# A graph-attention edge stream on one core: all source rows of a chunk gathered by GpSimd, none picked by TensorE

## The reference, cut to what matters

```python
h = (x_flat @ W_gat).reshape(M, HEADS, NUM_EXPERTS)        # M = 16384 nodes, 4 x 4
src = concatenate([edge_index[0], loops])                  # 262144 edges and 16384 loops
dst = concatenate([edge_index[1], loops])
a_src = (h * att_src).sum(-1);  a_dst = (h * att_dst).sum(-1)
e = leaky_relu(a_src[src] + a_dst[dst], negative_slope=0.2)
e_max = segment_max(e, dst);  ee = exp(e - e_max[dst])
denom = segment_sum(ee, dst)
alpha = ee / (denom[dst] + 1e-16)
agg = segment_sum(h[src] * alpha[:, :, None], dst) + b_gat
...
hh = gelu(x @ W1[ei] + b1[ei]);  out += g * (hh @ W2[ei] + b2[ei])   # four experts
```

## Time and profile before

| | us |
|---|---|
| median of 3 runs | 5086.44 (5078.35 to 5090.78) |
| profiled execution, span from first to last instruction | 5093.1 |
| PE busy | 3045.9 (60%) |
| DVE busy | 2806.7 (55%) |
| ACT busy | 2362.3 (46%) |
| POOL busy | 2224.4 (44%) |
| L937, the picking matmuls, x13056 | 1835.9 |
| L857, the gathers of the stream, x1632 | 1548.1 |

### The profile page before, as it was taken

How to read it: one execution, slowest core, us unless ns; L and a number is a source line. 1 busy time by engine, 2 the same in 40 slices (tenths; PEclk the granted TensorE clock), 3 DMA queues, 4 the chain that set the end, 5 groups by cost and what they waited for, 6 DMA issues and landing times. The chain is left out here.

```text
span 5093.1 us, 63233 instructions
## 1 busy us (share of the span) xinstructions
PE 3045.9 (60%) x21149; PEld 2318.6 (46%) x21149; DVE 2806.7 (55%) x5784; ACT 2362.3 (46%) x4288; POOL 2224.4 (44%) x2218
## 2 busy tenths in 40 slices
PE   3656663666566566566566566566566566544775
PEld 2445542554454454455455455455455455432443
DVE  8857883445445445445445445445445445467986
ACT  3636655444444444444444444444434434404886
POOL 7865613334434434434434434434434434426530
PEclk7657775777777777777777777777777777766887
DMA  1111101111111111111111111111111111112101
GB/s 58 24 22 20 22 7 44 24 23 27 31 23 27 31 23 27 31 23 27 31 23 27 31 23 27 31 23 27 31 23 27 31 23 27 25 27 75 38 19 33
DMA packets 157528, 145.13 MB, mean 28 GB/s; under 512 B 71240, under 2 KB 133080, under 8 KB 156776
## 3 DMA queue, kind: packets, MB, share of 16 engines
q1 hardware_dynamic: 88656, 109.49, 6.4%
q0 software_dynamic: 68768, 34.45, 6.2%
HBM read 92.97 MB, written 50.82 MB: 28 GB/s over the span
## 5 line engine op out<-in xcount | busy, mean ns | idle before, releaser
L937 PE MATMUL es_pgot<-hash_space,es_pick 128*128 128x256 bf16 x13056 | 1835.9, 288 | 1423.7 <-issue 1418.8
L857 POOL DMA_INDIRECT es_got<-node_table,late x1632 | 1548.1, 949 | 2127.0 <-DVEq L1077 1649.7
L937 PEld LDWEIGHTS es_pgot<-hash_space,es_pick 128*128 128x128 bf16 x13056 | 1302.8, 101 | 1899.6 <-issue 1742.7
L1019 DVE TENSOR_TENSOR es_prod<-es_pgot,es_own 128x512 f32<-128x512 f32 x272 | 187.7, 690 | 1801.6 <-PE es_pgot L937 1627.7
L871 ACT ACTIVATE es_pick<-es_away,consts 128x512 bf16<-128x512 f32 x1088 | 680.0, 711 | 7.0 <-DMA es_away<-sorted_keys 6.6
L293 POOL DMA_INDIRECT fr_ring<-in_emb,fr_rows x384 | 456.0, 1188 | 209.8 <-issue 112.8
L875 ACT ACTIVATE es_pick<-es_pick,consts 128x4096 bf16<-128x4096 bf16 x136 | 503.6, 3703 | 0.9
L894 ACT ACTIVATE ex_hid<-ex_phid,weights 128x256 f32<-128x256 f32 x128 | 53.6, 470 | 692.7 <-PE ex_phid L944 692.3
L1039 DVE TENSOR_TENSOR es_hot<-es_iota,late 128x1024 bf16<-128x1024 f32 x272 | 331.7, 1219 | 33.4 <-DVE es_st L1079 25.7
L1040 DVE TENSOR_TENSOR es_hot<-es_iota,late 128x1024 bf16<-128x1024 f32 x272 | 330.2, 1214 | 0.0
L894 ACT ACT_TABLE_LOAD x32 | 41.1, 1283 | 559.2 <-PE ex_phid L944 559.2
(11 more groups left out here) (351 smaller groups left out, 4294.6 us busy)
## 6 DMA issues: line engine op xcount, KB each, us to landing
es_away<-sorted_keys SPq DMA_DIRECT2D x68, 512.0 KB
es_got<-node_table,late POOLq DMA_INDIRECT x1632
edge_states<-es_st SPq DMA_DIRECT2D x68, 384.0 KB
expert_outputs<-ex_y SPq DMA_DIRECT2D x64, 256.0 KB
bk_y<-expert_outputs SPq DMA_DIRECT2D x8, 2048.0 KB
fr_ring<-in_emb,fr_rows POOLq DMA_INDIRECT x384
out_dram<-h SPq DMA_DIRECT2D x4, 1024.0 KB, 5.1
late<-in_edges SPq DMA_DIRECT2D x1, 2048.0 KB, 9.3
```

The costliest lines, as they stand in the source:

```text
L857: pool.indirect_dma_start(out=got[:, r, k, :], out_offset=None, in_=table_dram, in_offset=bass.IndirectOffsetOnAxis(ap=src[:, n, k:k + 1]. ...
L937: mm = pe.matmul(p_got[:, q, c * 256:c * 256 + 256], pick[:, r, q // 2, k, at * P:at * P + P], parts[:, part, k], start=(k == 0 and part = ...
```

## The change

GpSimd gathers all 32 columns of each chunk. The picking goes away with all that served it: the table's parts and the four `split` calls in `front`, the index rows and their transfers through DRAM, ScalarE's one-hots, TensorE's `pair`, VectorE's `sides`, `take` and `scores`. The hash arrays of `front`, which lay in the space of the parts, now lie in the ring of embedding rows. VectorE waits for 32 landings of a buffer in place of 24. Everything else, in the remaining order, stays.

```diff
-pool_cols = lambda t: t.rearrange("p (n c) -> p n c", c=CH)[:, :, 0:GC]
-pe_cols = lambda t: t.rearrange("p (n c) -> p n c", c=CH)[:, :, GC:]
+by_chunk_cols = lambda t: t.rearrange("p (n c) -> p n c", c=CH)
...
-        low = hash_space[0:B]
+        rows = sb("rows", [P, TILES, 3], I32)
+        ring = sb("ring", [P, RINGS, 3, ST, D])
+        low = ring[0:B].rearrange("b r n t d -> b (r n t d)")
...
-            def split(j):
-
-                tiles = slice(j * 32, j * 32 + 32)
-                block_rows = tab[:, tiles, 0:16].rearrange("p (h k) f -> p k h f", k=BLOCKS)
...
-                    ch.step(v.tensor_scalar(src, pool_cols(key), M - 1, None, ALU.bitwise_and))
...
-                    ch.step(v.tensor_scalar(few, pe_cols(key), BLOCKS * P - 1, None, ALU.bitwise_and)); ch.settle()
-                    ch.step(v.tensor_copy(mem["within"], tmp[:, 0:ROWS_T])); ch.settle()
-                    ch.step(v.tensor_scalar(few, pe_cols(key), 10, SIDES - 1, ALU.logical_shift_right, ALU.bitwise_and)); ch.settle()
-                    ch.step(v.tensor_copy(side, few)); ch.settle()
+                    ch.step(v.tensor_scalar(src, by_chunk_cols(key), M - 1, None, ALU.bitwise_and))
...
-                    if r < loads:
-                        pause(sp, s_pick, i * 4 + r * 2 + 4, s_spent)
-                        load(i * 2 + r + 3, 1 - r)
...
-                for k in range(GC):
+                for k in range(CH):
                     pool.indirect_dma_start(out=got[:, r, k, :], out_offset=None, in_=table_dram,
...
-                    if r < picks:
-                        pause(act, s_away[r], i * 16 + 32, s_spent)
-                        pause(act, s_got_p, c * PAIRS + 2, s_spent)
-                        squares(r, 0)
...
-                    if r < pairs:
-                        pair(c + 1, 1 - r, 0)
                     if with_experts:
                         expert(c, 0)
                         expert(c, 1)
-                    if r < pairs:
-                        pair(c + 1, 1 - r, 1)
                     count(c, 0)
                     count(c, 1)
...
-                    pause(dve, s_landed[r], (i + 1) * (16 * GC), s_spent)
+                    pause(dve, s_landed[r], (i + 1) * (16 * CH), s_spent)
...
                     count(c, 0)
                     count(c, 1)
-                    if r < takes:
-                        sides(c + 1)
-                        take(c + 1, 1 - r, 0)
-                        take(c + 1, 1 - r, 1)
...
                     count(c, 2)
                     count(c, 3)
-                    if r < takes:
-                        take(c + 1, 1 - r, 2)
-                        take(c + 1, 1 - r, 3)
-                        scores(1 - r)
```

More of the change, by code:

```diff
@@ L590, in _ @@
             dve.sem_inc(s_sorted, 1)
-            src, side, keep, starts, drop, hi, lo = (mem[n] for n in ("src", "side", "keep", "starts", "drop", "hi", "lo"))
-            few = tmp[:, 0:ROWS_T].rearrange("p (n c) -> p n c", c=PC)
+            src, keep, starts, drop, hi, lo = (mem[n] for n in ("src", "keep", "starts", "drop", "hi", "lo"))
             def prepare(part):
@@ L777, in edge_stream @@
         ps = lambda name, shape: ctx.enter_context(nc.psum_tensor(name, shape, F32))
-        C, W, xts, parts = mem["C"], mem["W"], mem["xts"], mem["parts"]
-        src, side, keep, starts, drop, hi, lo, within = (mem[n] for n in ("src", "side", "keep", "starts", "drop", "hi", "lo", "within"))
-        away = sb("es_away", [P, 2, PC * P], F32)
+        C, W, xts = mem["C"], mem["W"], mem["xts"]
+        src, keep, starts, drop, hi, lo = (mem[n] for n in ("src", "keep", "starts", "drop", "hi", "lo"))
         hot = sb("es_hot", [P, 2, 2, OH, P], BF16)
[L782 to L786, removed]
         row0 = sb("es_row0", [P, ROW], F32)
@@ L862, in _, with turn @@
             a = nc.scalar
[L863 to L884 removed]
+            def turn(i, with_experts):
                 for r in range(2):
                     c = i * 2 + r
[L887 to L890 removed]
                     if with_experts:
@@ L922, in _ @@
             pe.matmul(counts, hot[:, 0, 0, 0, :], hot[:, 0, 1, 0, :], start=True, stop=False, skip_group_check=True).then_inc(s_used, 2)
-            for b in range(5):
-                n = min(P, ROWS_T - b * P)
-                mm = pe.transpose(p_got[:].rearrange("p q n -> p (q n)")[0:n, b * P:b * P + P], within[:, b * P:b * P + n], C("ident"))
-            mm.then_inc(s_turned_p, 1)
-            def pair(n, r, q, first=False):
-                if q % 2 == 0:
-                    pause(pe, s_pick, n * 2 + q // 2 + 1, s_spent)
-                if not first:
-                    pause(pe, s_taken, (n - 1) * PAIRS + q + 1, s_spent)
-                for c in range(2):
-                    at = (q % 2) * 2 + c
-                    for k in range(BLOCKS):
-                        for part in range(3):
-                            mm = pe.matmul(p_got[:, q, c * 256:c * 256 + 256], pick[:, r, q // 2, k, at * P:at * P + P], parts[:, part, k],
-                                           start=(k == 0 and part == 0), stop=(k == BLOCKS - 1 and part == 2))
-                mm.then_inc(s_got_p, 1)
             def expert(c, n):
```

118 lines of the change are left out of this document (14 added, 104 removed).

## The result

| | before, us | after, us | ratio |
|---|---|---|---|
| where it was first measured | 5088.33 (5078.35 to 5090.78) | 4757.34 (4742.07 to 4762.91) | 0.9349, 95% interval 0.9328 to 0.9371 |
| chip 15 | 3396.67 (3391.22 to 3398.72) | 4093.17 (4090.91 to 4094.34) | 1.2052, 95% interval 1.2032 to 1.2072 |

The first row is the answer to the prediction: faster by 6.5%, 331 us, where the forecast said 700. The second row came out of the experiments and changes what the first one means: on another chip of the same kind the same two kernels are both faster, and the change makes the program 20.5% slower.

The account below looks back on a forecast made before the run. The edge stream's ring of waits, rooted in TensorE's slow issue during gathers, was taken as the bound. 1380.5 + 68 T, with T = 44.3 us per chunk, gave 4393, less 6.7 for the median: 4386 us; 8-in-10 range 4085 to 5190.

Parts of the forecast that it names:

- The ring of waits with TensorE at its root: Edge stream: GpSimd waits for VectorE, VectorE for TensorE, TensorE for its own issue (1190 us); a chunk takes 54.4 us.
- a sign of a wrong mechanism: Edge stream: pauses with TensorE long idle, or issue gaps of VectorE's or ScalarE's own, would disprove the forecast's mechanism.
- The picks leave the ring: Per chunk TensorE loses 192 of 260 matmuls, ScalarE and VectorE their picking work; direct worth nothing, only leaving the ring.
- Eight more gathers: GpSimd per chunk: 8 more gathers of 1.25 us, a burst of 40.0 us in place of 30.0, the chunk's floor.
- The pause: Between gather bursts: 8.6 us in every second chunk, so two chunks take 88.6 us, 44.3 each.
- such a burst hides TensorE altogether, the buffer is freed early: With a head start, TensorE fits about 84 matmuls into 40 us, over the 68 needed; the next burst follows without pause.
- The 3.4 us until the return: In the pause: TensorE is back at full rate 3.4 us after the last gather.
- The 5.2 us behind the return: In the pause: TensorE's other 48 matmuls at 9.2 per us take 5.2 us.
- Rival 2: Head start never returns, TensorE's and ScalarE's work follows the gathers: T = 56.7 us, 5230 us, slower; chance 0.22.
- Outside the loop: Ahead of the stream: VectorE loses the table's splitting, 5 us saved, between 0 and 13; the stretch after the stream unchanged.
- Rival 1: Edge stream: TensorE isn't slowed any more, T = 40.1 us per chunk, 4101 us; chance 0.24.
- rival 3: Edge stream: gathers get dearer beside VectorE, 1.188 + 0.30 us each, T = 47.6, 4610 us; chance 0.04.

Follow-up runs that it names:

- e10: Changed kernel with 16 of the 32 gathers per chunk, other columns left as set at the start; 3373.9 us on held chip 6 (kernel before 5120.4).
- e12: Changed kernel with one of the eight matmuls of each group of counts, most counts missing; 4783.3 us on held chip 3 (kernel before 5104.5).
- e7: Changed kernel with 24 of the 32 gathers per chunk and no picks; 3415.2 us on open chip 11 (kernel before 3397.0).
- e9: Kernel before, picks kept, with five more gathers per chunk into a spare tile; 5554.5 us on held chip 6 (kernel before 5120.4).
- c1: Changed kernel as it stands, timed on open chip 15; 4093.2 us (kernel before 3396.7).
- c2: Kernel before as it stands, run for its trace on open chip 15; 3393.4 us.
- e11: Changed kernel without the semaphore increment behind each wait of the stream; 4786.7 us on held chip 3 (kernel before 5104.5).
- e14: Changed kernel with 16 gathers per chunk and a waited-for GpSimd addition behind each; 3396.3 us on open chip 7 (kernel before 3392.4).

## Why the prediction was right in sign and wrong in size

*What bounds the kernel before.* The ring of waits with TensorE at its root was there. That TensorE's issue is slow was half of it. The release of the buffer also hangs on signals of TensorE that come late while gathers are issued, shown in the changed kernel and in e10 by matmuls that were done 27 and 10 us before the engine that waits for them goes on. What the prediction took for a sign of a wrong mechanism came with it: GpSimd pauses while TensorE has long been idle (12.8 us ahead of 1814.83 in e10), and in merged bursts VectorE has gaps of its own (e12).

*The picks leave the ring.* Right. I priced them at nothing beside GpSimd's floor. By R they are worth 24.0 - 8.9 = 15.1 us per chunk on a held chip, and nothing on an open one (e7). The 15.1 is inferred: no run on a held chip has 24 gathers and no picks, so it rests on the line through 16 and 32 gathers.

*Eight more gathers.* 10.0 us expected; 8 x 1.277 = 10.2 measured (e9, e10). The change on a held chip is then 10.2 - 15.1 = -4.9 us per chunk, times 68 = -333. That the spans differ by 332.0 is no check of it, since R was worked out from them.

*The pause, the step that failed.* I took one pause of 8.6 us in two chunks, 4.3 each; the pauses of the changed kernel come to 9.7 each. The mistake was in "such a burst hides TensorE altogether, the buffer is freed early": the 84 matmuls that fit into a burst were counted, as if a matmul that is done were a signal that has arrived. The signals come late, many of them after the gathers. In the changed kernel all but four bursts, and in e10 all but three, end in a pause of their own; where bursts merge in whole (e12) or nearly (the 2.9 us in the changed kernel), the pause behind them is of 20 us. The 5.4 us per chunk missing from the forecast are 367 us, and the pauses make nearly all of it: 659 us, of which 63 x 0.3 would stand between gathers anyway, against 34 x 8.6 = 292 in the forecast. Some 15 us more stand behind the last gather (571.4 us from 4189.7 to the end, where the sum had 556). The parts of the pause were mis-sized too. The 3.4 us until the return were near in e10 (3.2), and 7.9 (changed kernel) and 9.5 (e12) behind merged bursts. The 5.2 us behind the return had only TensorE's matmuls in them, where the trace of e10 has Gelus and Exp beside VectorE's one-hots, and then its scans and products: 6.4. Rival 2 listed ScalarE's steps, and had the pause too dear by adding matmuls that are long done.

*Outside the loop.* The stream's first row was gathered at 829.10, and in the changed kernel at 824.29, 4.8 us earlier: the 5 us were right.

*The rivals.* Rival 1, TensorE not held, is what five of seven later chips do. It gives T = 40.1 and 4101 us; c1 took 4093, with a gather at 1.277 and not 1.25 and a stream that begins 68 us earlier. But I had compared it with a kernel before at 5088, and there that is 3397: the rival's time came true and its sign didn't. None of my cases had the effect itself come and go, so none could see that the change loses where it is absent. The rule of the Trainium skill named there ("Runtime: NRT & Kernel Launch", Instruction fetch mechanics) gives no stall within a pass of the loop. The open chips agree, with 368 matmuls in 40 us in c2; the held ones, with 15 in 40 us, don't. What spoke for rival 1, TensorE's many matmuls in the embedding stage, told nothing of it: that stage is held too. GpSimd waits there for TensorE's `fr_turned` for 78.5 us in the recorded trace, and for 6.0 in c2. Rival 2 (T = 56.7) and rival 3 (mean gather over 1.0 us; 948 ns measured) didn't come.

*Still open.* What holds the signals, and why only on some chips, or in some minutes. It isn't the increments (e11), nor the count of matmuls by itself (e12). Whether TensorE's sparse matmuls and its late signals have one cause isn't shown either; no run tests a late supply of instructions as a rival. Against it as the whole cause stands that VectorE's gaps in e12 come only ahead of instructions that wait: L924, which waits for nothing, follows 0.2 us behind the start of L923 in the merged burst as everywhere. Whether the density of the gathers decides, and whether an earlier release shortens R, no run on a held chip shows. No version here beats both kernels: the one before is best on open chips, the changed one on held ones.

## What to carry to other kernels

A matmul that has ended in the trace is not yet a signal that has arrived. Before work is counted as hidden under a burst of gathers, follow one signal from its sender's end to the start of the engine that waits for it, and see whether the two lie within the burst.

Where a trace has a stall that nothing in it explains, run the unchanged kernel on another chip, and again later, before building on the stall. Here the stall came on some chips and not on others, and a change that trades work of four engines for 8 gathers of 1.28 us gains 6.5% with it and loses 20% without it.

Two sizes of a suspected term (16 and 32 gathers) give its price and the rest in one subtraction, if both are run on one chip.

## What the runs showed of the hardware that was not expected

- The same kernel takes 3392 to 3397 us on five chips and 5105 to 5120 on two others, each time close to its own value, with a gather of nearly the same price: 1.25 us from one to the next inside a held burst, 1.27 to 1.28 on the open chips (c2, c1).
- On the held chips matmuls, and signals from TensorE to ScalarE and VectorE, are late while GpSimd issues indirect gathers: 27 us in one burst of the changed kernel (2523.3 to 2550.42), 39 us in the next (2563.99 to 2602.68), and 50.5 us where two bursts merge (e12, 2412.74 to 2463.24). They return 3.2 us after the last gather in e10, 9.5 in e12, and sometimes within the burst (2550.42, with gathers until 2552.15). VectorE's signals to TensorE are prompt at 2527 in the changed kernel.
- In e12's merged bursts VectorE's waits for its own steps are late too: 3.1, 4.0 and 4.7 us at 2430.91, 2435.71 and 2445.51. In the changed kernel the same rows have no gap at 2598 to 2602.
- The embedding stage, ahead of any of this, is slower there too: the stream's gathers begin at 825.5 us where c1's begin at 756.9. In it GpSimd waits for TensorE's `fr_turned` 12 times, 88.0 us in all, where c1 waits once, 6.5 us: the hold isn't of the edge stream alone.
- An addition of 128x256 on GpSimd takes 0.62 us between gathers in e14, beside VectorE's own work, and with its signal and wait adds 0.6 us to each gather's period.
